# Twelve blocks in two contexts on one Trainium2 core: how the jobs are dealt to the contexts, and the order of the steps

## The reference

```python
x = x + _L0_xattn_ref(_layernorm(x, axis=-1), ctx_768, ...)
x = x + _L0_attn_ref(_layernorm(x, axis=-1), ...)
x = x + _L0_ffn_ref(_layernorm(x, axis=-1), ...)
x = x + _L1_xattn_ref(ctx_768, _layernorm(x, axis=-1), mask_BxS2_bk0, ...)
...
x = x + _L3_ffn_ref(_layernorm(x, axis=-1), ...)
```

## Time and profile before

| | |
|---|---|
| time, median of 3 runs | 2608.11 us (2601.25 to 2614.97) |
| the profiled execution | 2616.77 us, span 2615.5 us |
| PE busy | 2331.4 us (89%) |
| DVE busy | 1702.6 us (65%) |
| ACT busy | 1340.3 us (51%) |
| POOL busy | 780.3 us (30%) |
| moved by DMA | 84.18 MB, mean 32 GB/s |
| mean granted TensorE clock | 0.963 of full speed |

### The profile page before, as it was taken

One profiled execution on the slowest core, in us unless ns is written; L12 is line 12 of the kernel. 1 busy time (PEld: TensorE's weight loads), 2 busy tenths in 40 slices (PEclk: granted clock), 3 DMA queues, 4 the chain that ended last, 5 costly groups with the idle time before them and its releaser, 6 DMA issues.

```text
span 2615.5 us, 62549 instructions
## 1 busy us (share of the span) xinstructions
PE 2331.4 (89%) x26728; PEld 1560.2 (60%) x26728; DVE 1702.6 (65%) x4776; ACT 1340.3 (51%) x2305; POOL 780.3 (30%) x684
## 2 busy tenths in 40 slices
PE   5899999888889998888898888889989888999999
PEld 2566666665545555555576667666645555566666
DVE  4866556667887667768676776666776665655432
ACT  3576445776344338777754444444433566555342
POOL 2322555554121331111012233321210112454434
PEclk8999999999899999999999999999998899999999
DMA  4001442000000000000000000010010000122323
GB/s 124 14 1 37 100 105 60 22 15 11 3 3 6 1 23 37 14 14 2 11 15 19 18 19 19 27 31 14 26 55 8 8 2 2 49 53 53 106 73 89
DMA packets 50454, 84.18 MB, mean 32 GB/s; under 512 B 9536, under 2 KB 24768, under 8 KB 49792
## 3 DMA queue, kind: packets, MB, share of 16 engines
q1 hardware_dynamic: 50176, 80.18, 11.1%
HBM read 77.54 MB, written 2.62 MB: 31 GB/s over the span
## 4 chain that ended last, share of the span: by engine, by line
PE 55%; DVE 22%; ACT 11%; POOL 5%; issue 4%; DMA 2%; SPq 1%; DVEq 0%; POOLq 0%; ACTq 0%
PE psum L938 6%; PE psum L896 5%; PE psum L900 5%; PE psum L1598 3%; PE psum L463 2%; DVE c_L3x_most L1718 2%; PE psum L1691 2%; ACT c_L2x_p L2015 2%; PE psum L471 2%; ACT c_L2x_p L2013 2%; PE psum L1588 1%; PE psum L1387 1%; PE psum L765 1%; PE psum L770 1%; PE psum L1437 1%
## 5 line engine op out<-in xcount | busy, mean ns | idle before, releaser
L471 PE MATMUL psum<-halves_held 128*128 128x512 bf16 x616 | 177.6, 402 | 4.1 <-DVE x_held L635 2.2
L885 POOL TENSOR_TENSOR c_L3f_h<-c_L3f_h,c_L3f_spread 128x512 f32<-128x512 f32 x96 | 120.6, 1283 | 140.6 <-DMA c_L3f_spread<-scratch 107.2
L928 DVE TENSOR_TENSOR c_L3f_h<-c_L3f_h,psum 128x512 f32<-128x512 f32 (+1 forms) x112 | 75.6, 685 | 106.0 <-PE psum L900 77.9
L914 ACT ACTIVATE c_L3f_h<-psum 128x512 f32<-128x512 f32 x112 | 64.7, 594 | 108.2 <-PE psum L896 89.2
L938 PEld LDWEIGHTS psum<-weights,c_L3f_h 128*128 128x128 f32 (+1 forms) x896 | 106.7, 192 | 19.8 <-issue 16.0
L938 PE MATMUL psum<-weights,c_L3f_h 128*128 128x128 f32 (+1 forms) x896 | 109.9, 277 | 1.4 <-POOL c_L3f_h L885 1.4
L471 PEld LDWEIGHTS psum<-halves_held 128*128 128x128 bf16 x616 | 56.1, 101 | 85.1 <-issue 42.1
L896 PE MATMUL psum<-c_L3f_xT,weights 128*128 128x512 f32 x208 | 105.0, 596 | 0.0
L900 PE MATMUL psum<-c_L3f_xT,weights 128*128 128x512 f32 x208 | 104.8, 594 | 0.0
L885 POOL TENSOR_TENSOR c_L0f_h<-c_L0f_h,c_L0f_spread 128x512 f32<-128x512 f32 x64 | 80.5, 1276 | 78.3 <-DVE c_L0f_h L928 50.0
L1598 PE MATMUL psum<-c_L3x_qx,c_L3x_kT 32*128 32x256 f32 x512 | 78.8, 428 | 23.2 <-DVE c_L3x_most L1718 15.7
(11 more groups left out here) (639 smaller groups left out, 6602.2 us busy)
## 6 DMA issues: line engine op xcount, KB each, us to landing
c_L0f_spread<-scratch SPq DMA_DIRECT2D x64, 256.0 KB, 5.3
c_L3f_spread<-scratch SPq DMA_DIRECT2D x32, 512.0 KB, 5.6
c_L2f_spread<-scratch SPq DMA_DIRECT2D x64, 128.0 KB, 3.0
c_L3f_spread<-scratch SPq DMA_DIRECT2D x64, 128.0 KB, 6.1
c_L0x_ctxT<-ctxT SPq DMA_DIRECT2D x8, 384.0 KB, 4.8
c_L1x_ctx<-ctx SPq DMA_DIRECT2D x16, 192.0 KB, 2.4
c_L2x_ctxT<-ctxT SPq DMA_DIRECT2D x8, 384.0 KB, 3.6
c_L3x_ctxT<-ctxT SPq DMA_DIRECT2D x8, 384.0 KB, 3.5
```

What stands on the lines that cost most here:

```text
L471: nc.tensor.matmul(j.psum[:, bank, :], j.half["ident"], j.half["take"], start=True, stop=True)
L885: nc.gpsimd.tensor_tensor(h, h, j.m["spread"][:, f, :], ALU.mult).then_inc(*j.up("mixed"))
L928: nc.vector.tensor_tensor(h, h, j.psum[rows, bank, 0:j.tok], ALU.mult).then_inc(*j.up("gated"))
```

## The change

Three things change: the plan, the order, and one wait.

The first context's jobs were 4 of each block, 8 of L1x, 7 of L2f and 5 of L3f; now they are 2 of L0x, 3 of L0a and of L0f, 8 of L1x and of L2f, 4 of L1a to L2a and of L3x, 5 of L3a and 6 of L3f. The second context takes the others: 6, 5, 5, 8, 4, 4, 4, 4, 8, 4, 3, 2. Before, both had 56 jobs; now 55 and 57. Within a block the groups are in rising order.

The order is another string with the same number of steps and of `+`; its digits sum to 512, where they summed to 616. In `pe_linear` the jobs of L2a wait for the job before to be done ahead of the fillers into bank 3.

```diff
--- before.py
+++ after.py
@@ -650,6 +650,8 @@
             put = t.matmul(psum[:, bank, n * P:(n + 1) * P], m["xT"][:, n * P:(n + 1) * P], j.weight(w), start=True, stop=True)
         put.then_inc(*j.up("keys"))
     yield
+    if heads == 16:
+        j.free_bank(t)
     pe_warm(nc, j, 3)
     t.wait_ge(*j.at("values", 1))
     t.wait_ge(*j.at("kx", 1))
...
@@ -2840,80 +2842,80 @@
 PLAN = (
-    "a1a0a7a6b0b2b1b6c2c0c6c3d5d2ddd7d6d4d9dee0e1e2e6f0f2f6f4g0g4g2g6h0h2h6h4i2i8i6i1iciai0j2j0j4j6k0k6k2k4l0l2l4l7l3",
-    "a2a4a3a5b3b4b7b5c1c5c4c7d1d3d0dad8dcdbdfe5e4e3e7f3f1f5f7g1g3g5g7h1h7h3h5i4i3i5i9i7ieidibifj1j5j3j7k3k1k5k7l1l5l6")
+    "a0a1b0b1b2c0c1c2d0d1d2d3d4d5d6d7e0e1e2e3f0f1f2f3g0g1g2g3h0h1h2h3i0i1i2i3i4i5i6i7j0j1j2j3k0k1k2k3k4l0l1l2l3l4l5",
+    "a2a3a4a5a6a7b3b4b5b6b7c3c4c5c6c7d8d9dadbdcdddedfe4e5e6e7f4f5f6f7g4g5g6g7h4h5h6h7i8i9iaibicidieifj4j5j6j7k5k6k7l6l7")
 
 ORDER = (
-    "qQddDDpdDlLdkqddDKDpdVPavagpAlGdPapAgppPvvDaAvkvDvpPaPLqdGQpDadPdKlpVVgaApgVppvvdVaVPAPvQkGADvvpPapDgAqdPaddDGPLplDKPaVV"
...
+    "dvqQDdDDVLpdDldkqKQDddpdlPadagpaPAgpAGppPvvDaDLAvkGDvvpPaPdpdPdalpVgVaAplKVgppvdvVakvdvvVPPAAGPApQGDPaDpDvLvavvaPavPkdpd"
...
```

More of the change, by code:

```diff
@@ L2848 @@
[L2848 to L2855, removed]
@@ new lines @@
+    "PvagcVDVgVcVcVpVdpVvGcaVpGPvpAgpkPLaPgvPDLAPADPAAPKPPKVVPcAcDPDDLVAgVVcAAVcvpPadd1pVbrDPdrlrpVVVpaVKpVpraVVvGrprVpavGPvp"
+    "ArLrPrrrrPrADdrrPArrPrrrcPbAsPAPsPasVVPpApsPasVgVApAVgAVcvgkvPgpgpaKDVPvgcVVVcVpVcVcVGcVpDGPpAaPavPDgPALPAAPLDAPDKPKPVVP"
+    "pA1PvgVAVDcAAVcVDvpPaDqdLDpVpbrpdrrarPrrKrrpvrprVarrrprdrlpvarVprrvparrdVcpbVsvpaVpVspVvaGpsVpsvGPdpAsaPvgPdAPgAPAgPkAPg"
+    "PgPagcVpVg+DPcAvDPgcBRDcRRRcRdRlRRcRRRPRRdRcRARcRRRRdCvBpPkdSdvPvadVpSpaSPaAPgqpLAplSadVGSvPdGPVDCGAaPKCgVdPGvPvAgkPVdPA"
@@ new lines @@
+    "ClvPvpAPdVGapVpaGPakPGpACvCvVaCGCvvCVPpAaPvDpBDRPDaRLRpRRRdvppaqdapRRRdRdpRRRARpRaRagRRRvRlaCPdvBgdPSVPAvSPvdgDdVPASKPVS"
+    "PklvPASvpAVppaGPaaPGVPAGpVGCvCGvaPGPvvPApAPavdVpdGCakpvpapqvdpaddVpagpaGvCladCdgCvCvdgCVPADPvPDBv1pRRppRARPRaRDaRPRaRdRl"
+    "kRpRVALRPRvPRvRaRRRRVCPBvvSdpASPavVpSPakSpvpadpqvDpaGpaSAGpagCGvadCVgCGvPvPgAPVdPAKPvPdvAlpVpGapdaPadGPAdkVpVGdCvGCvaClC"
+    "dvvCVPpADaPvPdDBpRRRPRaRkRRpRRRRRRRvpPappRDRALRpRaRRdaCDVpagvBASddPaSPVgvPASlvPvdVgkqPAPVSPAPGVSdPAGdKCvVPGdvppGapaPalAC"
@@ new lines @@
+    "VPGpAGCvGCvddaCCkvvPpVaCGvpCaVPpAQDvpPDvdpBPaRRaRpRRRRpaRRRDRpLRRgRRAaRPRaRRRvCgPVBSPvAdvPDdDgSVPADPVSPAlvSPdvpVSpapaPAG"
+    "qaPGpCGvPvdGaCdVCdGvvPlpAACavkDVpLKddGPakpPvdpAVPavGppadpdaDVgpaGCladCvkgCKvCvgV+VPPqADAPvQPADvpDGpdapaPdADdVlaVLpAvGvVa"
+    "DVdGvv9pVa1PkvPVpdADDPaApAvppadPaDdKLpVdpVavAgplaVvDadV7PKgvAvDgVPA3PkvvVPppapaQPaApAPvPvDaPvv1pVDDavpaApAGvdpLa3pDvAVDG"
+    "pvpvvvgpdvgVVDaGvvDpgVL4PvPAvpVpdPalApAaPapVpVdAv7pvVvV4PvvAKvpkDV2pPapAaPappvvvDv8pvpadpVpvPvAKQvvgPDpADgPvaDvLPpDvVKdp"
@@ new lines @@
+    "dDAPAvGgAlvpVG1paVpVDGdaappV1PvPAvpADvLVvDPvA3PkDvpVpaVApaVVapp2PvvvvpvpVa2pKddpdvAPvA1PvpvgvgpVPPAPQDVavPDvApAPAvGgAlDv"
+    "pVG1paLVpVDDGaappV1PvPAvpAvDDVLvPvA3PKvpVpaVDApaVVapp2PvvdvkvDpKvpAa1pdVpvPvAPvpvgVPQDPAgvPDDVLavPpDdvdDApAPAvGADpvG1pla"
+    "VVpVGaappV1PvPA1pKvvVAvDLPvgA2PdvpVpaVApaVVapkp1PvvAvv1pVPvDdpAvdPaKpvvVDQPvaPaAvvAvPvdvVlvvPAvvDGvPvADvvDvLvvvvvpaApvGV"
+    "pVvpaVDDGdkppavVVPpgpvagpaPvPAApgApvpgppvvvpPapvvvVaavvvvvvVvAvvvvvvvvvvVpVavKDpdPdvvdvlpDpapaApvVgdpapvgpLaPvkDgpApvpgp"
@@ new lines @@
+    "pvvvp1PaKpvvvdaavvvvDvVPPAAPvQPvAvDvGDvPAvvvvvVvvvpDdLavApDvGDpVdVpDaVvGpaplVDvpLVPvgPAPApgaApaPvgpVpdVvApgpKVDV3PKApVkP"
+    "vvADvpPqVPPADAPVdPAdGdDPADaLVlpAvGvvaVaVvGvvvvvvvvvvvvvvvvVp1PvvDVPAPaApAvPvpVdVpaKpapvAgpVVapvgPApVaPpAPpVv+PVgpvADkPgD"
+    "pVpPvPvvVqpVVGpavVGVpGAVvagPPv4pVVPadPnAPzAmdzDdzlAPwgyPL3nwwVxVPVVyDmVnxymVPxKdnmzPzwAnwkPzA1mzzAPwy9nwwx2myPxnVmynx1mz"
+    "zVnwVwVmzPwzVPAwzPPwyVxnVPVVy1mGDnxVGVymnx1mGAPzznwwVmzPzzwy9nwwVx1myDVPxDnmynxzmz1PwwApa1pvpqPapAvAgpvPaPdpVaVPVLVnVmgz"
@@ L2919 @@
+    "PgPRRRBRpRRPRRARCaPBvSpVAgSpapSvPgaPVSPAPVSGpAGPPVGvPAgPVPAGPVGPAPGVPAGPVPGAPVPGAPVPGAPVpGApaPvpVPGaPvAPVcAcVccccccccccc"
+    "cCvsCCCCCCCCCCCCCVS")
 class Flow:
```

108 lines of the change are left out of this document (47 added, 61 removed).

## The result

| | before | after |
|---|---|---|
| time, median of 6 runs each | 2607.55 us (2600.06 to 2614.97) | 2624.11 us (2616.32 to 2629.12) |
| ratio after / before | | 1.0067, 95% interval 1.0046 to 1.0087 |
| profiled execution, its span | 2616.77, 2615.5 us | 2616.38, 2615.1 us |
| PE busy less fillers | 2153.8 us | 2164.0 us |
| N (span less that) | 461.7 us | 451.1 us |

The change makes the kernel 16.5 us slower; 44 us less were forecast. The two profiled executions took the same time: that of after (2616.38 us) is among the fastest of its six, that of before (2616.77) is slower than all six in the table. They also ran at nearly the same mean granted clock, 0.964 and 0.963, while the six runs of after have a mean of 0.959.

What follows compares the result with a forecast made beforehand. TensorE was taken as full where both contexts are in expert blocks, elsewhere chains hopping between engines leave it gaps. Terms -30.6 - 16.8 - 11 + 10 + 4 = -44 us gave 2564 us from the median 2608.1; range 2492 to 2640.

Steps and rivals of the forecast that it cites:

- item 3: Newly mixed stages with no full partner, some 1100 us: gain of 1%, -11 us, bounds 0 and -33.
- item 1: L0f beside L0a and L1x jobs: L0f fills their TensorE gaps, -30.6 us, bounds 15 and 32.
- item 2: L3f at the end, now also beside 2.5 L3x jobs: TensorE full, -16.8 us, bounds 8 and 18.
- items 4 and 5: 35 more table loads on ACT, +10 us (0 to 45); weights of L2x and L2f loaded later, +4 us (0 to 13.7).
- The estimate by the Trainium skill: Adds a drain of about 1380 ns to each ACT table load: +21 us on the path, time 2575 us.
- The wait: Wait for the job before in pe_linear for L2a: 0, or 4 us if the fillers' place matters.
- 104 fillers fewer: Fillers on TensorE cut from 616 to 512: 0 by themselves, at most -30 us.
- Rival D: Slower by the clock where TensorE has gaps: at a mean of 0.93 +71 us, some 2635 us; chance 0.21.
- Rival C: Gains cancel: L0f no faster beside others, mixtures 0, loads and weights cost up to 45; 2600 to 2621 us; chance 0.17.
- B: The middle gains too: L1a beside L1x eases shared shortages, 42 us more go, about 2520 us; chance 0.15.
- A: The forecast itself: full stages grow, faster by 25 to 75 us, 2533 to 2590 us; chance 0.47.

Runs made afterwards that it cites:

- the hybrids: The two kernels with the new plan and order in one part only, otherwise as before: apart_at_start, ratio 0.9959, and apart_at_end, 1.0025.
- apart_at_start: New plan and order through L0, then 11 L1x jobs for the first context and on as the kernel before, new wait included: 2595.04 us, ratio 0.9959.
- apart_at_end: Kernel before up to each context's fifth L2f job, then 11 L2f jobs for the second and the new order's end, new wait included: 2615.26 us, 1.0025.

## Why the prediction was wrong

The time lies inside the range (2492 to 2640), as the range was wide, and 60 us above the forecast; the sign is wrong. The step that failed is item 3, which booked the newly mixed stages without a full partner as a small gain: measured, they lose. Of the 60 us it is 33 (-11 forecast, +22 by the hybrids); item 1 is 20 and item 2 some 23, and 14 come off that items 4 and 5 had set aside as costs. By its items:

1. *L0f gets company, -30.6.* Too large: -9 us in the trace (N -14.4, work +5.5), -11 by `apart_at_start`. The mark was 320 us with N under 15; it was 331 with N = 331 - 315.67 + 2.54 = 17.9. The 23 more table loads of this part do not explain the shortfall: without any load its last job ends at 491.7 us in place of 493.3. L0f did not run at 36 us but at 41 beside L1x: four intervals from 329.5 to 492.6.

```profile
L1063 DVE TENSOR_TENSOR x_held<-x_held,psum x5: 680/689/690, 329.5 to 492.6; 128x512 f32<-128x512 f32 x5
```

   The saving is near the lower bound (15) that the prediction gave for L0f at 47 us. That it fits is luck in part: 0.86 and 0.92 of TensorE over 5.8 x 27 us and some 94 us leave 22 + 8 = 30 us of N, not 16, so the bound should have been some 2. L3f beside L3a showed that TensorE gets full, not that an L0f job alone can use 64% of it; at 41 us it used 57%.
2. *L3f gets more company, -16.8.* Nearly right for its own stretch: 440.1 us with N of 5.2 + 6.3 = 11.5, forecast 440 and under 10. But the place of it was too narrow. To have L3f beside L3x, L3a has to stand beside L2f and L3x, and there N is 23.0 of 124 us and 37.6 of 139. The whole tail comes to N -9.3 in the pair and to +6.5 us by `apart_at_end`.
3. *Other mixtures, 1%, -11.* The step that failed. The middle is +13 of N in the trace and +22 us or more by the hybrids. The 1% was taken from one row with a partner's row on each side, L2f with L3x. That mixture did win again (1653 to 1912: N is 259 - 233.11 + 14.93 = 40.8, while four L2f at 5.1 and four L3x at 7.1 are 49), but it does not stand for L1a with L1x, 52.6 against 41, nor for L2x with L1a, 70.9 against 62. The bound "0" at the upper end said that a mixture can't be worse than its parts. Nothing in the trace gave a reason for that, and it is false. The stage with the most N of all, L2x with 90 us, is not among the rows that the prediction prices from.
4. *Table loads, +10.* Count right (35 more). The price can't be called wrong: the gap between the kernels shrinks by 8 to 10 us without loads, with an interval from nearly nothing to 20. The way to it, a fifth of ACT's time on the path, is not borne out: by it the 149 us of the 116 loads of before would be worth some 30 us, and they were worth 0. The estimate by the Trainium skill ("ScalarE: Activation LUTs", "What ACT_TABLE_LOAD costs"), +21, lies just outside that interval, and this trace does not show the drain: the load in the earlier trace rows starts at 2257.32 us, 0.01 us after the activation before it ends, and the next activation starts 0.02 us behind it.
5. *Weights, +4.* Nothing. The first matmul of L2x follows after 0.53 us of idle time:

```profile
816.19 1.96 PE L1877 MATMUL psum<-c_L2x_ctxT,weights 96*128 96x512 f32 x4 [0.53 <-issue]
```

   22 steps ahead of it were enough. Ahead of the first matmuls of L2f (1184.79 us in the same trace) TensorE has no idle time either.
6. *The wait.* 0, as said: 1.0003.
7. *104 fillers fewer.* As a count nothing that shows: a gap of 16 us is there without any filler too.

The work was to stay at 2153.8 within 20: 2164.0, right. N was to fall to 418: 451.1.

Rival D, slower by the clock, was priced from 0.942 down, at 21 us for each 0.01. The mean clock was 0.969 in twelve runs of before (the fillers' session; 0.967 to 0.970 in the others) and 0.959 in the six of after. Between runs of before the time goes with the clock at some 14 us for each 0.01, so this alone is 14 of the 16.5 us; and the profiled pair, at equal clocks, took equal times. D had the direction and named what moved. Its price was half too high, and its point of 0.942 far too low, because it was set against the full 44 us: the pair at equal clock has 10.6 us less N, and 10.2 us more work with it. (That the time goes with the clock from run to run does not say which of the two makes the other.) But the clock is not the cause by itself: the kernels without fillers have the same clock (0.897 and 0.899) and keep a gap, which there stands in N (373.1 and 392.0). That the mixed stages leave TensorE other gaps, and that the kernel pays for them in idle time without fillers and in clock with them, fits all these figures; no run isolates it. Rival C had a part right, item 1 at half and item 3 at nothing, and its 45 us of loads and weights far too high; B had the wrong sign. The prediction's own figure for A, 2533 to 2590, is 18 to 75 us less than before, not the "25 to 75" that it says.

What makes L1a beside L1x slow is only argued here. Neither engine time nor a transfer is short in it. By the ends of the jobs an L1a job takes 39 us and an L1x job some 43, where they take 48.5 and 27 among their like, so the two contexts keep no common rhythm. `ORDER` fixes every engine's queue, so a late step of one context can hold up the other's. No run isolates that.

## What to carry to other kernels

A mixture of two stages that both leave gaps is not bounded by the sum of its parts; price it from a row of just that mixture, or give it a range that reaches to a loss (here 11.6 of 156 us in one stretch, 9 of 223 in another). Before a plan is changed throughout, change it at one place and join the known order behind it: here the start alone gives 0.41%, with more fillers 0.69% (2588.75 us, faster than both kernels), and the whole plan loses 0.67%. An order that is better by measured durations is a guess until its clock column is seen.

## What the runs showed of the hardware

- 616 matmuls whose results nobody reads are worth 95 us in before: without them the mean granted clock is 0.897 instead of 0.969 and 2153.8 us of work become 2329.7.
- Between runs of one program the time goes with the granted clock: 19 runs of before lie between 2596.26 us at 0.975 and 2619.71 at 0.964, and a straight line fitted through them has some 14 us for each 0.01 (14 to 16 in the three other sessions). On that line before would take 2623 us at 0.960, the time of after at its own 0.959.
- More fillers are not better by themselves: with 209 more the clock of after was 0.964 instead of 0.959, and the time was no better (2634.31 us for 2624.11, intervals of the ratios overlapping).
- 151 loads of activation tables, 193 us of ACT, moved the time by some 9 us, in intervals that just overlap; 116 loads, 149 us, by nothing that could be measured.
